# Embedding look-ups on TensorE: hot ids made local floats a fill ahead and compared with constants, third layer moved behind the next group's first look-up

## The reference

```python
e = jnp.stack([tbl_0[ids[:, 0]], ..., tbl_26[ids[:, 26]]], axis=1)   # (2048, 27, 128)
xactions = jnp.einsum('bfd,bgd->bfg', e, e)
z = xactions[:, _TRIL_I, _TRIL_J]                                     # 351 pairs
h = jnp.concatenate([z, dense_ctx], axis=1)                           # 367
h = jnp.maximum(h @ W_top1 + b_top1, 0.0)                             # 512
h = jnp.maximum(h @ W_top2 + b_top2, 0.0)                             # 256
y = h @ W_top3                                                        # (2048, 1)
```

## Time and profile before

| | us |
|---|---|
| median of 3 runs | 420.1 |
| lowest and highest | 419.85, 423.21 |
| the profiled execution | 421.49 |
| its span in the trace | 419.6 |

### The profile page before, as it was taken

The page is one execution under the profiler, slowest core; times in us unless marked ns, Lnnn a source line. Parts: engine busy times, 40 slices in busy tenths (PEclk is TensorE's granted clock), DMA queues, the critical chain, the costliest instruction groups (busy, mean ns, idle before and its releaser), DMA issues.

```text
span 419.6 us, 14576 instructions
## 1 busy us (share of the span) xinstructions
PE 366.5 (87%) x6180; PEld 323.4 (77%) x6180; DVE 302.3 (72%) x996; ACT 210.4 (50%) x435; POOL 275.4 (66%) x286
## 2 busy tenths in 40 slices
PE   0858669899898999999899998899899998999788
PEld 0757559898698878898698977888688986998565
DVE  2999968993689837995589936996479935891320
ACT  3446263745435482635526573634617463564822
POOL 4777777777777778777777778777775777400020
PEclk9999969999899999999899999999999998999989
DMA  7974362242232423233232422223231421100000
GB/s 276 339 229 143 90 209 77 60 123 66 70 85 58 135 57 84 57 89 105 77 84 58 134 59 84 59 65 126 68 93 36 116 54 51 41 10 5 5 10 5
DMA packets 19601, 37.70 MB, mean 90 GB/s; under 512 B 6792, under 2 KB 8400, under 8 KB 19536
## 3 DMA queue, kind: packets, MB, share of 16 engines
q0 software_dynamic: 8896, 17.89, 16.4%
q1 hardware_dynamic: 8704, 16.00, 11.5%
q10 hardware_dynamic: 1936, 2.89, 2.1%
HBM read 35.88 MB, written 0.01 MB: 86 GB/s over the span
## 4 chain that ended last, share of the span: by engine, by line
PE 39%; DVE 36%; ACT 16%; issue 6%; DMA 3%; SPq 1%; ACTq 0%; DVEq 0%
DVE one_hot L633 29%; PE fill_ps L430 9%; PE mlp_ps L460 9%; PE pair_ps L447 8%; PE fill_ps L431 8%; ACT et L540 7%; ACT work L330 6%; DVE work L330 5%; DMA work<-tbl_d 3%; PE fill_ps L413 1%; PE fill_ps L475 1%; DVE table_lo L620 1%; PE mlp_ps L493 1%; PE mlp_ps L486 1%; ACT table_hi L533 1%
## 5 line engine op out<-in xcount | busy, mean ns | idle before, releaser
L391 POOL DMA_INDIRECT rows<-tbl_d,ids_sb x272 | 271.4, 998 | 89.8 <-issue 80.8
L633 DVE TENSOR_SCALAR one_hot<-hot_ids,chunk_row 128x256 fp32r<-128x256 int32 x720 | 220.3, 381 | 3.2 <-PE fill_ps L431 2.5
L430 PE MATMUL fill_ps<-one_hot,table_hi 128*128 128x256 f32 x720 | 191.5, 302 | 27.2 <-DVE one_hot L633 25.3
L431 PE MATMUL fill_ps<-one_hot,table_lo 128*128 128x256 f32 x720 | 183.2, 290 | 0.0
L430 PEld LDWEIGHTS fill_ps<-one_hot,table_hi 128*128 128x128 f32 x720 | 143.2, 199 | 40.4 <-issue 21.7
L431 PEld LDWEIGHTS fill_ps<-one_hot,table_lo 128*128 128x128 f32 x720 | 143.7, 200 | 0.0
L330 DVE COPY work<-pair_ps 26x112 f32<-26x112 f32 (+1 forms) x256 | 66.1, 258 | 66.4 <-PE pair_ps L447 63.2
L330 ACT COPY work<-pair_ps 26x112 f32<-26x112 f32 (+1 forms) x256 | 60.9, 238 | 94.4 <-PE pair_ps L447 91.7
L540 ACT COPY et<-fill_ps 128x512 f32<-128x512 f32 (+1 forms) x80 | 78.0, 1100 | 0.4
L552 ACT COPY et<-fill_ps 128x512 f32<-128x512 f32 x40 | 46.4, 1213 | 60.2 <-PE fill_ps L431 51.0
L447 PE MATMUL pair_ps<-et 128*26 128x26 f32 x4096 | 52.9, 193 | 9.8 <-issue 5.5
(11 more groups left out here) (21 smaller groups left out, 60.3 us busy)
## 6 DMA issues: line engine op xcount, KB each, us to landing
hot_ids<-ids_hot_d SPq DMA_DIRECT2D x34, 256.0 KB, 3.9
rows<-tbl_d,ids_sb POOLq DMA_INDIRECT x272
work<-tbl_d SPq DMA_DIRECT2D x4, 640.0 KB, 4.1
work<-tbl_d SPq DMA_DIRECT2D x4, 512.0 KB, 7.4
hot_ids<-ids_hot_d ACTq DMA_DIRECT2D x6, 256.0 KB, 7.3
w_sb<-w_d ACTq DMA_DIRECT2D x1, 768.0 KB
w_sb<-tbl_d SPq DMA_DIRECT2D x1, 640.0 KB, 4.2
w_sb<-tbl_d SPq DMA_DIRECT2D x1, 512.0 KB, 12.1
```

The costliest lines, as they stand in the source:

```text
L391: nc.gpsimd.indirect_dma_start(out=rows[:, t, c, :], out_offset=None, in_=tables[f], in_offset=bass.IndirectOffsetOnAxis(ap=ids_sb[:, tile ...
L430: nc.tensor.matmul(to, table_hi[:, CHUNK_AT[k] + c, :], hot, start=(c == 0), stop=False)
L431: last = nc.tensor.matmul(to, table_lo[:, CHUNK_AT[k] + c, :], hot, start=False, stop=(c == CHUNKS_OF[k] - 1))
L633: last = nc.vector.tensor_scalar(one_hot[:, (first + c - c0) % ONE_HOT_RING, :], hot_ids[:, slot, (k - k0) * COLS:(k - k0 + 1) * COLS], ch ...
```

## The change

There are two parts.

The first is in how one-hots are made. Before, `chunk_row` had a column for each chunk of each table width (18), computed once from an iota. Now `first_row` has one column per width, width * partition. A new step on VectorE, `localise_ids`, subtracts it from the ids of a hot fill, in place, and writes the result as float: the id counted from the partition's first row. It is one instruction where both tables of the fill have the same width, else two: 6 per group, 4 of 128x512 and 2 of 128x256. It is done one fill ahead, behind the one-hots of the first table of the fill before. The one-hots are then compared with the constant float(c), and their source is float. They wait on `hot_ids_local` where they waited on the load.

The second is the place of layer 3 in STEPS: layer 3 of b now stands behind fill 0 of group b + 2, ahead of pairs 2 of group b + 1; that of group 6 stands between the last two pair steps.

```diff
--- before.py
+++ after.py
@@ -85,10 +85,11 @@
             steps += hot[:3] + cold[0] + hot[3:] + [("pairs", g, 0)] + cold[1][:2] + [("pairs", g, 1)] + cold[1][2:]
         else:
             b = g - 1
-            steps += [hot[0], ("pairs", b, 2), hot[1], ("pairs", b, 3), hot[2]] + cold[0][:2] + [hot[3]] + cold[0][2:4]
+            steps += [hot[0]] + ([("layer3", b - 1)] if b > 0 else [])
+            steps += [("pairs", b, 2), hot[1], ("pairs", b, 3), hot[2]] + cold[0][:2] + [hot[3]] + cold[0][2:4]
             steps += hot[4:] + cold[0][4:] + [("layer1", b), ("pairs", g, 0)] + cold[1][:2]
-            steps += [("layer2", b, 0), ("pairs", g, 1)] + cold[1][2:] + [("layer2", b, 1), ("layer3", b)]
-    return steps + [("pairs", GROUPS - 1, 2), ("pairs", GROUPS - 1, 3)]
+            steps += [("layer2", b, 0), ("pairs", g, 1)] + cold[1][2:] + [("layer2", b, 1)]
+    return steps + [("pairs", GROUPS - 1, 2), ("layer3", GROUPS - 2), ("pairs", GROUPS - 1, 3)]
 
 
 STEPS = order()
@@ -126,6 +127,17 @@
 
 PARTS = one_hot_parts()
 PART_ENDS = [first + halves(k)[half][1] - halves(k)[half][0] for (_, k, half), (_, first) in PARTS.items()]
+
+
+def runs_of(step):
+
+    k0, n = hot_fills(step[1])[step[2]]
+    widths = CHUNKS_OF[k0:k0 + n]
+    return [(w, widths.index(w), widths.index(w) + widths.count(w)) for w in sorted(set(widths))]
+
+
+def localised_through(n):
+    return sum(len(runs_of(step)) for step in list(HOT_FILL)[:n + 1])
 
 
 def parts_through(step):
@@ -228,8 +240,8 @@
         table_hi = sb("table_hi", [P, ALL_CHUNKS, DIM], F32R)
         table_lo = sb("table_lo", [P, ALL_CHUNKS, DIM], F32R)
         one_hot = sb("one_hot", [P, ONE_HOT_RING, COLS], F32R)
-        chunk_row_int = sb("chunk_row_int", [P, sum(WIDTHS)], I32)
-        chunk_row = sb("chunk_row", [P, sum(WIDTHS)])
+        first_row_int = sb("first_row_int", [P, len(WIDTHS)], I32)
+        first_row = sb("first_row", [P, len(WIDTHS)])
         ident = sb("ident", [P, P])
         et = sb("et", [P, COLS, FEATURES])
         w1_sb = sb("w1_sb", [P, CHUNKS, HIDDEN1])
@@ -262,7 +274,8 @@
         hot_used = sem("hot_used")
         consts = sem("consts")
         ident_ok = sem("ident_ok")
-        chunk_row_ok = sem("chunk_row_ok")
+        first_row_ok = sem("first_row_ok")
+        hot_ids_local = sem("hot_ids_local")
         cold_full = sem("cold_full")
         fill_moved = sem("fill_moved")
         pair_full = sem("pair_full")
@@ -366,11 +379,9 @@
 
         @block.gpsimd
         def _(pool):
-            at = 0
-            for width in WIDTHS:
-                nc.gpsimd.iota(chunk_row_int[:, at:at + width], pattern=[[1, width]], base=0,
+            for n, width in enumerate(WIDTHS):
+                nc.gpsimd.iota(first_row_int[:, n:n + 1], pattern=[[0, 1]], base=0,
                                channel_multiplier=width).then_inc(consts, 1)
-                at += width
             nc.gpsimd.memset(ident[:, :], 0.0).then_inc(ident_ok, 1)
             pool.wait_ge(ident_ok, 1)
             nc.gpsimd.affine_select(out=ident[:, :], in_=ident[:, :], compare_op=ALU.not_equal, fill=1.0, base=0,
@@ -609,8 +620,8 @@
         @block.vector
         def _(dve):
             dve.wait_ge(consts, len(WIDTHS))
-            nc.vector.tensor_copy(chunk_row[:, :], chunk_row_int[:, :]).then_inc(chunk_row_ok, 1)
-            dve.wait_ge(chunk_row_ok, 1)
+            nc.vector.tensor_copy(first_row[:, :], first_row_int[:, :]).then_inc(first_row_ok, 1)
+            dve.wait_ge(first_row_ok, 1)
 
             def make_low(k):
 
@@ -620,19 +631,28 @@
                 nc.vector.tensor_tensor(table_lo[:, c0:c1, :], raw_table(k), table_hi[:, c0:c1, :].bitcast(F32),
                                         ALU.subtract).then_inc(lo_made, 1)
 
+            def localise_ids(step):
+
+                slot = HOT_FILL[step] % IDS_RING
+                dve.wait_ge(hot_ids_in[slot], 16 * (HOT_FILL[step] // IDS_RING + 1))
+                for width, k0, k1 in runs_of(step):
+                    ids = hot_ids[:, slot, k0 * COLS:k1 * COLS]
+                    n = WIDTHS.index(width)
+                    nc.vector.tensor_scalar(ids.bitcast(F32), ids, first_row[:, n:n + 1], None, ALU.subtract
+                                            ).then_inc(hot_ids_local, 1)
+
             def make_one_hots(step, k):
 
                 slot = HOT_FILL[step] % IDS_RING
                 k0 = hot_fills(step[1])[step[2]][0]
-                at = sum(WIDTHS[:WIDTHS.index(CHUNKS_OF[k])])
-                dve.wait_ge(hot_ids_in[slot], 16 * (HOT_FILL[step] // IDS_RING + 1))
+                ids = hot_ids[:, slot, (k - k0) * COLS:(k - k0 + 1) * COLS].bitcast(F32)
+                dve.wait_ge(hot_ids_local, localised_through(HOT_FILL[step]))
                 for half, (c0, c1) in enumerate(halves(k)):
                     part, first = PARTS[step, k, half]
                     wait_count(dve, hot_used, parts_in_the_way(first + c1 - c0))
                     for c in range(c0, c1):
-                        last = nc.vector.tensor_scalar(one_hot[:, (first + c - c0) % ONE_HOT_RING, :],
-                                                       hot_ids[:, slot, (k - k0) * COLS:(k - k0 + 1) * COLS],
-                                                       chunk_row[:, at + c:at + c + 1], None, ALU.is_equal)
+                        last = nc.vector.tensor_scalar(one_hot[:, (first + c - c0) % ONE_HOT_RING, :], ids,
+                                                       float(c), None, ALU.is_equal)
                     last.then_inc(hot_made, 1)
 
             def output(g):
@@ -644,11 +664,14 @@
                 k0, n = hot_fills(step[1])[step[2]]
                 return range(k0, k0 + n)
 
+            localise_ids(("hot", 0, 0))
             for step in HOT_FILL:
                 if step[1] == 0:
                     for k in tables_of(step):
                         make_low(k)
                         make_one_hots(step, k)
+                        if k == tables_of(step)[0]:
+                            localise_ids(NEXT_HOT[step])
             dve.wait_ge(lo_made, MOST_HOT)
             nc.vector.memset(zt, 0.0).then_inc(zt_clear, 1)
             dve.wait_ge(zt_clear, 1)
@@ -657,6 +680,8 @@
                     following = NEXT_HOT[step]
                     for k in tables_of(following):
                         make_one_hots(following, k)
+                        if k == tables_of(following)[0] and following in NEXT_HOT:
+                            localise_ids(NEXT_HOT[following])
                 elif step[0] == "pairs":
                     _, g, bank = step
                     if bank == 0:
```

## The result

The changed kernel takes 399.9 us in the median (396.3 to 401.6, and one run of 415.2), against 420.9: a ratio of 0.946, with a 95% interval from 0.937 to 0.956. The forecast was 391, a ratio of 0.931, in a range of 381 to 414. So the sign, the range and most of the size held, and a quarter of the gain was missing. The run of 415.2, over 1.5% above the fastest, is left out of the ratio. The profiled execution took 398.1, with a span of 396.2, where the forecast for the span was 389.6.

The account below looks back on a forecast made before the run. TensorE was taken to bind, held up by one-hots and layer 3, with GpSimd's gathers the second bound. Savings of 34 us were capped at 29.6; with 0.3 at the tail, 30 us off gave 391, range 381 to 414.

Parts of the forecast that it names:

- The one-hot, 0.200 us apart, 0.246 with hold-ups: VectorE's 720 one-hots: spacing falls from 0.263 to 0.200 us, or from 0.309 to 0.246 with hold-ups.
- Localising, 2.6 to 3.0 us per group: Six new VectorE instructions per group that subtract from the ids: 2.6 us, 3.0 with hold-ups.
- VectorE stops binding, 2.2 us per group: Fills 3 and 4 of the look-ups no longer wait for one-hots, so TensorE binds there: 2.2 us per group.
- Layer 3 covered, 1.8 us per group: Moved layer 3 stands behind 32 matmuls, 3.9 us, which cover TensorE's wait for its activation: 1.8 us per group.
- The half-clock stretches go with it, 6.4 us: Four stretches of halved TensorE clock behind the layer-3 gap vanish with the idle time: 6.4 us in all.
- The start, 3 us: Up to about 50 us VectorE is the chain: 5.7 us saved on one-hots, 2.6 added by localising, 3 us gained.
- TensorE's own sum, 34 us: Total saving over the whole kernel if TensorE alone bound, before the limit set by gathers: 34 us.
- The gathers' cap: GpSimd's gathers limit the gain: last transposes move from 391.2 to 361.6, so 29.6 us can go.
- last issue ended at 360, landed 1.6 later: End of GpSimd's gathers: with 2 to 3 us of relief the last rows land in time for transposes at 361.6.
- Overlong gathers, which may stay: GpSimd's gathers beyond 0.944 us each, 14.7 us in all over 272 gathers, taken as possibly unchanged.
- rival C: Quicker one-hots on VectorE lock GpSimd's gathers out: 20 us slower, 440, or more; chance 0.11.
- Rival A: VectorE's one-hot doesn't get cheaper, while localising is still paid: 418 us, nearly no change; chance 0.10.

Follow-up runs that it names:

- the fourth experiment: The changed kernel with localised ids written back as int32 and compared with the constant: 409.2 us (406.9 to 412.0), ratio 0.975 to before.
- its first part alone: The changed kernel with layer 3 back in its old place, so only the one-hots are new: 402.9, 413.1, 418.3 and 418.5 us, against 419.4 before.

## Why the prediction was right or wrong

- *The one-hot, 0.200 us apart, 0.246 with hold-ups.* Right: 0.202 and 0.232. That the middle between "nothing" and the memset's fixed part came out so close is luck: the reckoning took away the pointer and the integer source together, and the runs show that the pointer alone made the difference. The Trainium skill's formula (VectorE: DVE Perf Modes, the section on the TRN2 errata) gives an estimate of 194 ns for 256 elements, 4% under the 0.202 of these runs. The pointer's 0.061 us (0.263 less 0.202) on top of it gives 0.255, against the 0.263 of before.
- *Localising, 2.6 to 3.0 us per group.* Right: 2.65. It is paid back only because the pointer goes.
- *VectorE stops binding, 2.2 us per group.* Right: fills 3 and 4 run without a gap.
- *Layer 3 covered, 1.8 us per group.* Right: its wait is gone.
- *The half-clock stretches go with it, 6.4 us.* Right for the four behind layer 3, wrong for the sum. Time short of full clock is (1 - 0.972) x 419.6 = 11.7 us before and (1 - 0.974) x 396.2 = 10.3 after: 1.4 us came back net, because stretches at 35.8 and 148.4 came, each behind a wait for rows, and the one around 57 us grew. With only layer 3 moved, where no rows are waited for, it is (1 - 0.983) x 405.2 = 6.9.
- *The start, 3 us.* Better than that at first: the first pairs begin at 47.3 us instead of 51.7. The waits for one-hots there fell by 5.2 us, and 3.7 us of waiting for rows came in their place.
- *TensorE's own sum, 34 us.* Not shown. One group was 42.7 us long, near the 43 that this sum comes to, but 34 gathers need 42.5 as well, and no run let TensorE alone bind on chip A.
- *The gathers' cap.* The mechanism was right: TensorE now waits for rows, and GpSimd is on the chain. Its size is the step that was off, "last issue ended at 360, landed 1.6 later". The last gather began at 363.5 and ended at 364.4, 4.4 us later than that, and TensorE took its rows 2.9 us after that end instead of 1.6: 367.3 instead of 361.6. (The page of the kernel before has no landing time for gathers; the 1.6 was that of GpSimd's plain copies. In the changed kernel gathers landed 2.5 to 3.3 us after their start.) That is 5.7 of the 6.6 us by which the span missed. The other 0.9 is the tail: 28.9 us from the last transposes to the end, where it was 28.4 in the earlier trace rows, and where I expected 0.3 less. The place was off too. I looked for the cap only at the end of the run; on the chain the gathers bind in the first 54 us and at places up to 276 us, and no longer at the end.
- *"Overlong gathers, which may stay."* They grew, from 14.7 to 19.5 us, and in the first 55 us from 2.8 to 8.7. I took relief from a faster start, which came (waits for TensorE fell from 5.2 to 2.4), and never charged the quicker one-hots to the gathers in the likeliest case, though rival C said it.
- *Rival C.* Its mechanism is real, and I put it wholly on the other side of the forecast, as if it were absent or ruinous. On chip A overlong gathers grew by 5 us in the changed kernel and by 15 with integer ids and constant. The Trainium skill (SBUF — State Buffer, section on its two separate sides) says a VectorE instruction that uses both ports holds GpSimd off for its whole length, and one with two SBUF inputs does so to a GpSimd instruction that reads SBUF. The runs here go further, since gathers were shut out by up to 55 instructions in a row; that these one-hots use both ports is not shown. The rival's point of decision, 0.1 us per gather, is where the whole gain would be gone. It doesn't mean that less costs nothing: a mean gather 0.039 us longer (1.055 against 1.016) made the fourth experiment 10.8 us longer than the changed kernel.
- *Rival A* comes to the time of the kernel with the pointer kept: 415.9, against 418.
- *A small slip.* The two groups of the earlier trace rows differ by 48.64 - 46.92 = 1.7 us, not 1.6.

That 391 was missed by only 9 us is in part luck: too much was counted for the clock and too little for the gathers, and the cap hid the first.

What I can't settle is the spread of the changed kernel and of its first part alone (396 to 415, 403 to 418). The profiled execution of the latter, 413.1, lost 14.0 us in early gathers, 11 more than before, and 413 less 11 is close to its lowest, 403. That would account for it, but one trace is not enough to call it shown.

## What to carry to other kernels

When a wait is removed from the engine that binds, look at the engine that never waits: how far it is ahead, at the start as well as at the end, is all that can be gained, and its own margin must be charged with what the change does to it. A [128, 1] operand of a short VectorE instruction can cost a quarter of it; shift the data so that a constant will do. But long runs of such instructions beside gathers issued by GpSimd can shut the gathers out; a break every few instructions kept them short here, and whether it pays has to be measured.

## What the runs showed of the hardware

- A per-partition operand costs a 128x256 tensor_scalar 0.06 us: 0.263 against 0.202 apart. Float or integer source makes no difference: 720 one-hots are busy 223.4 and 220.3 us with the pointer, 166.7 and 165.3 without it.
- A gather that takes 0.944 us took 4.9 to 13.7 beside unbroken VectorE work, with or without pointers. In the first 55 us the three kernels without the pointer lost 8.7 to 20.3 us in this way, the three with it 2.8 to 4.9. VectorE waiting for its own last instruction every 4 or 5 one-hots kept all gathers under 2.3 us in three executions, on chips B and C; but on chip A the kernel with float ids and pointer stayed under 2.2 without any break.
- On three of four chips, all used after the first, the kernel before took 589 to 599 us instead of 420, and on one of them the changed kernel 602 instead of 400. In the changed kernel TensorE got its instructions there in small portions, 0.72 or 1.44 us apart, and each gather left out gave back 1.4 us, in it and in the kernel before. A change that gains 5% on one chip lost 2% on another.
